# Selective scan in a chain of half-units: a ring of six buffers instead of five, and TensorE's sums three half-units behind the scan instead of two

## The reference, cut to what matters

```
def step(h, inp):
    dt_t, B_t, C_t, u_t = inp
    dA = jnp.exp(dt_t[:, :, None] * A)
    h = h * dA + (dt_t * u_t)[:, :, None] * B_t[:, None, :]
    y = jnp.einsum('bdn,bn->bd', h, C_t)
    return (h, y)
_, ys = jax.lax.scan(step, h0, seq)
y = jnp.transpose(ys, (1, 0, 2)) + u * D_param
y = y * jax.nn.silu(z)
```

## Time and profile before

| | us |
|---|---|
| median of 3 runs | 2120.67 |
| lowest and highest | 2118.75, 2123.79 |
| the profiled execution's own time | 2122.75 |
| its span, first to last instruction | 2121.0 |
| first scan of chunk 0 to last scan of chunk 11 | 73.2 to 1460.8 |
| DVE busy, share of the span | 1822.9, 86% |
| PE busy, share of the span | 1739.7, 82% |

### The profile page before, as it was taken

The page is one execution under the profiler, slowest core; times in us unless marked ns, Lnnn a source line. Parts: engine busy times, 40 slices in busy tenths (PEclk is TensorE's granted clock), DMA queues, the critical chain, the costliest instruction groups (busy, mean ns, idle before and its releaser), DMA issues.

```text
span 2121.0 us, 23810 instructions
## 1 busy us (share of the span) xinstructions
PE 1739.7 (82%) x8210; PEld 651.4 (31%) x8210; DVE 1822.9 (86%) x2159; ACT 1211.9 (57%) x2171; POOL 1147.5 (54%) x585
## 2 busy tenths in 40 slices
PE   5788879678797888678788888796897899999985
PEld 2222213132231323232322222232663333333323
DVE  4699999899999999999998999999547888888803
ACT  3766465645656666555565666543452266666672
POOL 2688877877888887789898787764000000000000
PEclk9898979869697899899997999887998799999998
DMA  6152522222223232322222232331061522220001
GB/s 198 56 160 79 95 71 75 66 61 71 75 70 98 79 95 80 87 70 72 91 81 88 74 100 73 108 90 46 1 121 39 83 33 32 32 32 2 2 2 40
DMA packets 95941, 149.83 MB, mean 71 GB/s; under 512 B 24291, under 2 KB 31651, under 8 KB 95412
## 3 DMA queue, kind: packets, MB, share of 16 engines
q1 hardware_dynamic: 95820, 148.31, 27.1%
HBM read 137.05 MB, written 10.62 MB: 70 GB/s over the span
## 4 chain that ended last, share of the span: by engine, by line
PE 40%; DVE 34%; issue 9%; POOL 8%; ACT 7%; DMA 2%; SPq 0%; DVEq 0%; ACTq 0%; POOLq 0%
DVE hbuf L2331 19%; DVE hbuf L2312 7%; PE psum L1721 6%; PE psum L731 6%; POOL hbuf L1421 6%; PE psum L697 5%; PE psum L717 4%; PE psum L612 3%; PE psum L1510 3%; DVE gain L1012 2%; PE psum L601 2%; PE psum L1673 1%; PE psum L1518 1%; PE psum L1537 1%; DMA cbuf<-scr_c 1%
## 5 line engine op out<-in xcount | busy, mean ns | idle before, releaser
L1421 POOL TENSOR_TENSOR hbuf<-hbuf,cbuf 128x1024 f32<-128x1024 f32 x384 | 901.8, 2358 | 272.9 <-DVE hbuf L2331 141.2
L2119 ACT ACTIVATE psum<-slots,cols 128x512 f32<-128x512 f32 x708 | 485.5, 689 | 392.0 <-DVE hbuf L2331 387.9
L1721 PE MATMUL psum<-hbuf,ident 64*64 64x512 f32 x3072 | 491.6, 715 | 172.8 <-POOL hbuf L1421 172.2
L2312 DVE TENSOR_TENSOR hbuf<-slots,psum 128x1024 f32<-128x1024 f32 x354 | 422.1, 1193 | 49.8 <-POOL slots L1338 30.3
L2331 DVE TENSOR_TENSOR_SCAN hbuf<-psum,hlast,hbuf 128x512 f32<-128x512 f32 x354 | 432.5, 1263 | 8.7 <-ACT psum L2119 8.7
L2331 DVE TENSOR_TENSOR_SCAN hbuf<-psum,hbuf 128x512 f32<-128x512 f32 x354 | 411.1, 1200 | 8.8 <-ACT psum L2119 8.8
L1012 DVE TENSOR_REDUCE gain<-psum 128x1 f32<-128x512 f32 x512 | 315.4, 680 | 59.2 <-PE psum L697 58.7
L563 POOL COPY wl<-hbuf 128x512 f32<-128x512 f32 x8 | 4.8, 613 | 429.1 <-PE psum L731 400.4
L697 PE MATMUL psum<-slots 99*128 99x512 bf16 x512 | 197.1, 400 | 23.9 <-DVE gain L1012 11.5
L717 PE MATMUL psum<-slots 102*128 102x512 bf16 x512 | 194.5, 388 | 6.5 <-ACT xn_flat L895 1.7
L1721 PEld LDWEIGHTS psum<-hbuf,ident 64*64 64x64 f32 x3072 | 91.0, 147 | 318.3 <-POOL hbuf L1421 255.4
(11 more groups left out here) (278 smaller groups left out, 2234.3 us busy)
## 6 DMA issues: line engine op xcount, KB each, us to landing
cbuf<-scr_c SPq DMA_DIRECT2D x384, 256.0 KB, 3.2
slots<-scr_qk SPq DMA_DIRECT2D x96, 128.0 KB
wl<-scr_diag SPq DMA_DIRECT2D x18, 256.0 KB, 4.7
scr_qk<-slots SPq DMA_DIRECT2D x8, 512.0 KB, 2.8
wl<-in_w SPq DMA_DIRECT2D x8, 496.0 KB, 4.9
wl<-in_ada_w SPq DMA_DIRECT2D x1, 3584.0 KB
xt<-in_x SPq DMA_DIRECT2D x2, 1024.0 KB, 12.5
wl<-in_w SPq DMA_DIRECT2D x2, 1024.0 KB, 7.0
```

What stands on the lines that cost most here:

```text
L1421: pool.tensor_tensor(hs, hs, cbuf[:, at % CRING:at % CRING + 1, :].to_broadcast([P, 2, TC]), ALU.mult).then_inc(weighed, 1)
L1721: last = pe.matmul(psum[side, bank, :], ident[rows_of, rows_of], hbuf[rows_of, at % RING, q, :], start=False, stop=n == NS - 1, skip_group ...
L2119: act.activation(decay_bank(at, q), dts[k % 2][:, e, :], ACT.Exp, scale=coefficient(WORK[k], e, n)).then_inc(decay, 1)
L2312: dve.tensor_tensor(hbuf[:, at % RING, :, :], ws[k % 2][:, 2 * p:2 * p + 2, :], psum[:, 2 + at % 2:3 + at % 2, :].to_broadcast([P, 2, TC]) ...
```

## The change

The ring gets a sixth buffer, PE adds half-unit `at - 3` instead of `at - 2`, and four kinds of instruction move by one slot with it: DVE's gate and ACT's `keep_sums` (from slots 1 and 17 to 2 and 18), and ACT's evictions of `u` (from slots 19, 19, 21, 21 to 20, 20, 22, 22). No computing instruction is added or removed. The whole diff:

```diff
-RING = 5
+RING = 6
+LAG = 3
@@
-                    if at >= 2:
-                        add_state(at - 2)
+                    if at >= LAG:
+                        add_state(at - LAG)
@@
-            for at in range(TOTAL - 2, TOTAL):
+            for at in range(TOTAL - LAG, TOTAL):
                 add_state(at)
@@
-                        yield (19, 19, 21, 21)[e]
+                        yield (20, 20, 22, 22)[e]
                         if e == 0:
                             act.wait_ge(summed, HALVES * (k - 1) + NS + 1)
@@
-                    if h == 1 and j and j - 1 not in GATED:
+                    if h == LAG - 1 and j and j - 1 not in GATED:
                         keep_sums(j - 1, 1)
-                    if h == NS + 1 and j not in GATED:
+                    if h == NS + LAG - 1 and j not in GATED:
                         keep_sums(j, 0)
@@
-                    if h == 1 and j - 1 in GATED:
+                    if h == LAG - 1 and j - 1 in GATED:
                         gate(j - 1, 1)
-                    if h == NS + 1 and j in GATED:
+                    if h == NS + LAG - 1 and j in GATED:
                         gate(j, 0)
```

## The result

The changed kernel takes 2131.34 us (median of 5 runs, 2130.43 to 2136.9) against 2120.67 before (5 runs): ratio 1.0045, 95% interval [1.0024, 1.0066], slower by some 9.5 us by the ratio (10.7 by the medians) where 13.4 less were forecast. Its profiled execution took 2136.9 (span 2135.2); it is the longest of the five, and 14.2 of span more than before. First scan to last scan grew from 1387.6 to 1401.5 us, so 13.9 of these lie in the twelve chunks, and none in the attention.

What follows compares the result with a forecast made beforehand. DVE was taken as the bound, idle only 48.2 us in the chunks' 1388 us. Gains of 15.3 less 1.9 gave 13.4 us, so 2109.3 for the profiled execution and 2107.3 for the median, range 2100 to 2119.

Steps and rivals of the forecast that it cites:

- Ring and lag: DVE's load waits: gains of 3.3 us in chunk 1, 0.7 in chunk 2, 3.1 at chunk ends, 0 elsewhere.
- Chunk 1: Slot 13, load waiting 5.28 us after a slow DMA held POOL: 2.0 us left, gain 3.3, bounds 0 and 5.3.
- product waits: Scans waiting for PE's products by matmul, 6.4 us: gain 4.6, bounds 2 and 6.4; under 2.5 us left in total.
- (b): Rival, PE behind at most gates, all chunk starts included: slower by 6.5 us, 2127; chance 0.08.
- Evictions of u: One slot later, into slots where ACT has room: 0 us, bounds -3 and +1.
- keep_sums: One slot later: gain 1.6 us in chunks 6 and 10, 1.7 in chunk 9.
- Gates: Gate, skip product, forward result one slot later: loss 1.9 us in chunk 11; chunks 7 and 8 together gain 0.3.
- The sum: Whole kernel: gains of 15.3 us less a loss of 1.9, giving 13.4 us faster.
- (a): Rival, DVE's waits move to ACT's decays instead of going: about 3 us gained, 2118; chance 0.20.
- (c): Rival, PE leaves half clock in chunks 1, 3, 4 and 9: 21 us gained, 2099.5; chance 0.10.
- The prediction's own test: Forecast wrong if scans wait for ACT at slots 3 or 23 of many chunks, or DVE's chunk idle exceeds 42 us.
- The clock: PE's long idle gaps would come more often by the skill's rule: 1.7 us less gained, 2109.0.

Runs made afterwards that it cites:

- combined kernel: Changed kernel with u's evictions at slots 20, 20, 21, 21, conversions ahead of keep_sums, two side pieces in slot 18 of the last chunk: 2108.36 us, ratio 0.9931.
- u back: Changed kernel with ACT's last two evictions of u behind slot 21 instead of 22: 2121.14 us, ratio 0.9987 to the kernel before.
- u alone: Kernel before with only u's evictions moved to slots 20, 20, 22, 22 from 19, 19, 21, 21: 2135.93 us, ratio 1.0061.
- ring alone: Kernel before with six ring buffers and nothing else changed: 2122.92 us, ratio 1.0008.

## Why the prediction was wrong

*Ring and lag:* right in kind. Chunk 1 was forecast to keep 2.0 us and kept 2.40, but the other six kernels with ring six and lag three keep nothing there, so the match is partly luck; chunk 2 changed its releaser; the load waits of slot 1 in chunks 7, 8, 9 and 11 went; product waits fell to 1.4 (under 2.5 forecast). The spreads' total stayed at 12.6, forecast 7: 4.1 of it are new ones of place 1, and chunks 3 and 4, forecast to stay at about 4, have 5.7. In the combined kernel it is 1.9. Two small slips of the prediction change nothing: the wait left in chunk 1 comes to 1.9 from its own numbers, and the gains of keep_sums to 3.3, not the 3.4 of rival (b). The "5 us waits of PE" that it names are loads' waits; PE's wait in the earlier trace rows is 7.77.

*Evictions of u:* this step failed, and it decided the sign. I put 0 with a bound of 3 us of loss, "cover is PE's own backlog", and none of it DVE's; it cost 12 us (u back) or 13 (u alone). PE had no such backlog: seven times it was on time for `xp` and stood, 10.1 us in all, waiting for ACT's eviction. I followed the data (`xp` reads u's blocks) and not the bank, and did not list what ACT has queued behind its copy of `xp`.

*keep_sums:* the mechanism was half right. I counted ACT's work up to the end of slot 2 as unchanged, and a slot gained; but it stood behind a later PE sum. Forecast 1.6 + 1.7 gained; the gaps rose by 4.4 instead, 7.7 apart. For chunk 9 the text named the two side pieces ahead of the sum, and its wait stayed at 3.3 as that bound had it; the same reason held in chunks 5, 6 and 10 and wasn't applied there. The 3.4 us of chunk 9 from which 1.7 were taken also aren't a fixed property of the old order, as the runs of the ring alone and of u alone show (0.24 and 0.21).

*Gates:* chunk 11's place and mechanism were right, the size was 3.3 us in the gaps and not 1.9, as the idle PE came back at a lower clock (0.60 granted from 1426 to 1430 us). Chunk 7 showed 3.2 more us of gaps, and chunk 8's wait of 0.97 stayed, where the two together were to gain 0.3. Of the 3.2, 1.21 is a wait of DVE for PE's piece L1487 that all seven kernels with ring six and lag three have, and none of the others; the other 2.0, at the load of slot 6, is there in some of the seven and not in others, and what sets it is open. The stake was larger than I thought: at the old lag the slot of gate and keep_sums alone is worth 41 us.

*The sum:* 13.4 forecast, less 12 (u), 7.7 (keep_sums) and 1.4 (chunk 11), is a loss of 8, or 11 with 3.5 for chunks 7 and 8; the ratio says 9.5. The term of u is from times and the others are gaps of one profile, so this gives their order of size and no more. With u back and the two side orders mended, the same ring and lag give 0.9931 of before, some 14.6 us less. That this is near the forecast's 13.4 is in part luck: in the gaps of the combined kernel chunk 1 gained 5.3 (forecast 3.3), chunks 3 and 4 gained 2.7 (forecast 0), chunk 7 lost 3.0, and the 3.6 gained at slots 2 and 3 need an order that the forecast didn't have.

*The rivals:* (a) came nearest in kind, since the waits moved to ACT, but at places that the change itself made; (b) had the sign and a total of 6.5 us, with keep_sums in it, but its main term, gates at all chunk starts, is not in the trace. (c), an end of half clock, did not happen. The prediction's own test, scans waiting for ACT at slots 3 or 23, was met at slots 3 and 24.

*The clock:* mean granted clock in the chunks fell, and PE's busy time rose with as many matmuls; before and after, 73 us on:

```profile
73.00:1461.00 1388.00, 1132.95 (x5251) 388.28 (x5249) 1341.65 (x1275) 823.82 (x1451) 1115.62 (x542) 0.87 0.30 83
```

```profile
73.00:1476.00 1403.00, 1175.05 (x5255) 401.76 (x5257) 1344.56 (x1276) 821.75 (x1451) 1116.68 (x542) 0.84 0.29 82
```

PE's waits for POOL fell by 127.0 us, its waits for DVE rose by only some 80, and its busy time by 42.1.

This is the direction that the prediction took from the Trainium skill, page "TensorE: Matmul & The Clock Gate", section "HAM oscillation — how this bites in real kernels", where idle gaps drop PE to half clock. But the fastest kernels here have it too (combined: 0.84, PE busy 1174.45 us), so the lower mean clock by itself doesn't explain the loss; places 1 and 3 show it at work where something is queued behind PE. What is left of it is open: within one kernel the slower executions have the lower mean clock (23 executions of the kernel before on one chip, 0.875 to 0.893, correlation with the time -0.75), and no run here tells whether the clock makes the time or the time the clock.

## What to carry to other kernels

When a stage is moved, list for each moved instruction not only who reads its data but who reuses its buffer, and what stands behind each of these waiters on its engine: here an eviction one slot later held a matmul that read none of its data, through the PSUM bank two groups on. In a slot where an engine waits for another's late result, put the work that is ready ahead of the wait; work that isn't ready there wins nothing. Judge a change with several moves by parts: here ring and lag gained, and what the moves that went with them did to the queues turned it into a loss.

## What the runs showed of the hardware

An idle gap of PE of only 1.9 us can be followed by matmuls at the lower level. In chunk 9 of the changed kernel the granted clock is 1.00 from 1204 to 1208 us, then comes the gap's end at 1208.26, it is 0.50 from 1208.5 to 1211.5, and 1.00 from 1212 on. The half of `xp` behind the gap takes 3.65 us instead of 1.96, so that a wait of 1.92 us cost 3.6 in PE's time. It doesn't always happen: with u back, PE waited 1.80 us until 1182.69, and the granted clock is 1.00 from 1180 to 1193.
